# Scatters of half rounds, each half with its own semaphore, and GpSimd's wait two halves back

## The reference

```python
h = relu(layernorm(x));  x = x + rel_gnn(h, 8 relations)      # REL
h = relu(layernorm(x));  x = x + edge_attention(h, 4 heads)   # ATT
h = relu(layernorm(x));  x = x + sage2(h)                     # SAGE0, SAGE1
h = relu(layernorm(x));  x = x + gcn(h)                       # GCN

# the part that all of them share
msg = f(h)[src]                                    # a row per edge
agg = segment_sum(msg, dst, num_segments=50000)    # summed by destination
out = g(h) + agg                                   # a row per node
```

## Time and profile before

| what | value |
|---|---|
| median of 3 runs | 4481.74 us (4466.53 to 4487.24) |
| profiled execution | 4498.36 us, its span 4496.7 us |
| SAGE0's stretch with scatters | 2413 to 2806 us |
| SAGE1's | 3219 to 3688 us |
| GCN's | 4084 to 4480 us |
| busy: PE, DVE, ACT, POOL | 65%, 56%, 43%, 55% |
| packets of SyncE's queue | 233406, 34.5% of the 16 DMA engines' time |
| packets of GpSimd's queue | 90944, 13.2% |

### The profile page before, as it was taken

The page is one execution under the profiler, slowest core; times in us unless marked ns, Lnnn a source line. Parts: engine busy times, 40 slices in busy tenths (PEclk is TensorE's granted clock), DMA queues, the critical chain, the costliest instruction groups (busy, mean ns, idle before and its releaser), DMA issues.

```text
span 4496.7 us, 81538 instructions
## 1 busy us (share of the span) xinstructions
PE 2929.0 (65%) x19724; PEld 2566.6 (57%) x19724; DVE 2499.0 (56%) x11513; ACT 1955.0 (43%) x5394; POOL 2473.3 (55%) x2379
## 2 busy tenths in 40 slices
PE   6888887774656563004767777566777665777666
PEld 5887886663555553003655555466666554666666
DVE  5666667885555453883324555323466563445666
ACT  2222325664544442113546555223444444556555
POOL 5565553666788886445554555545444435554444
PEclk9999998998877776556888676778888887889989
DMA  4444436875333333992113767211277771114767
GB/s 160 157 166 156 163 127 192 239 239 157 41 41 41 41 41 75 313 310 77 38 36 112 229 218 220 71 31 34 86 245 239 230 241 49 37 38 137 221 216 220
DMA packets 328251, 638.77 MB, mean 142 GB/s; under 512 B 61072, under 2 KB 89776, under 8 KB 321992
## 3 DMA queue, kind: packets, MB, share of 16 engines
q1 hardware_dynamic: 233406, 501.99, 34.5%
q0 software_dynamic: 90944, 133.85, 13.2%
q10 hardware_dynamic: 3786, 1.65, 0.1%
HBM read 371.35 MB, written 277.50 MB: 144 GB/s over the span
## 4 chain that ended last, share of the span: by engine, by line
PE 16%; DMA 13%; issue 11%; POOL 10%; another core or an unknown queue 4%; DVE 4%; ACT 3%; SPq 0%; POOLq 0%; DVEq 0%; ACTq 0%
DMA sums<-parked,last_i 12%; POOL sums L774 9%; PE bank L1201 6%; PE bank L1197 3%; PE bank L1185 3%; PE bank L1167 2%; DVE out_stats L1665 1%; PE bank L1137 1%; ACT e_h L911 1%; DVE out_mv L1672 1%; ACT out_sd L1072 1%; ACT psum_out L948 1%; DVE n_t L1765 0%; POOL got L739 0%
## 5 line engine op out<-in xcount | busy, mean ns | idle before, releaser
L774 POOL DMA_INDIRECT sums<-parked,last_i x588 | 603.5, 1026 | 702.6 <-DMA sums<-parked,last_i 506.4
L739 POOL DMA_INDIRECT got<-rows,gidx x588 | 602.7, 1025 | 404.8 <-ACT e_h L911 188.4
L948 ACT ACTIVATE psum_out<-bank 128x132 f32<-128x132 f32 x784 | 219.7, 280 | 939.3 <-remote 455.0
L1201 PE MATMUL bank<-psum_out,eq 128*128 128x132 f32 x1568 | 387.2, 332 | 246.0 <-ACT psum_out L948 154.6
L1033 ACT ACTIVATE n_h<-ring 128x128 f32<-128x128 f32 x1176 | 482.9, 482 | 143.7 <-DMA ring<-rows 71.2
L1302 PE MATMUL bank<-ring,ident 128*128 128x128 f32 x2352 | 507.6, 302 | 0.0
L1201 PEld LDWEIGHTS bank<-psum_out,eq 128*128 128x128 f32 x1568 | 271.2, 216 | 306.4 <-ACT psum_out L948 181.9
L1299 PE MATMUL bank<-w_t,n_ht 128*128 128x128 f32 x1568 | 355.7, 353 | 136.1 <-DMA ring<-sums 135.3
L1277 PE MATMUL bank<-ident,n_h 128*128 128x128 f32 x1176 | 226.9, 324 | 330.9 <-ACT n_h L1033 248.2
L1182 PE MATMUL bank<-parked 128*128 128x128 f32 x3136 | 409.7, 283 | 32.7 <-issue 26.1
L1182 PEld LDWEIGHTS bank<-parked 128*128 128x128 f32 x3136 | 386.9, 199 | 41.4 <-issue 40.6
(11 more groups left out here) (182 smaller groups left out, 7292.4 us busy)
## 6 DMA issues: line engine op xcount, KB each, us to landing
ring<-sums SPq DMA_DIRECT2D x392, 264.0 KB
ring<-rows SPq DMA_DIRECT2D x392, 264.0 KB
rows<-ring SPq DMA_DIRECT2D x294, 264.0 KB
ring<-attsums SPq DMA_DIRECT2D x98, 264.0 KB
rowsg<-ring SPq DMA_DIRECT2D x98, 264.0 KB
ring<-rowsg SPq DMA_DIRECT2D x98, 264.0 KB
sums<-parked SPq DMA_DIRECT2D x16, 1584.0 KB
attsums<-parked SPq DMA_DIRECT2D x16, 1584.0 KB
```

The lines of the kernel that those rows point to most:

```text
L739: pool.indirect_dma_start(out=got[:, b, j, 0:width], out_offset=None, in_=table[:, :], in_offset=bass.IndirectOffsetOnAxis(ap=gidx[:, b, j ...
L774: pool.indirect_dma_start(out=sums[:, :], out_offset=bass.IndirectOffsetOnAxis(ap=last_i[:, t:t + 1], axis=0), in_=parked[:, t, :], in_off ...
L948: nc.scalar.activation(psum_out[:, b, j, :], bank[4 + j % 2][:, 0:W], ACT.Copy)\
L1201: nc.tensor.matmul(o, lhsT=eq[:, b, j, 1, :], rhs=carried, start=False, stop=True)\
```

## The change

The scatter of a round is split in two halves of two tiles. Each half has a semaphore of its own (`half_scattered[0]`, `half_scattered[1]`), which counts 32 for each landed half. GpSimd issues the first half of a round, waits for the second half of the round before, issues the second half, and waits for the first. `rounds_landed` is counted when a round's second half has been waited for. The indices, the data and the number of DMAs are the same, and at most two halves are under way, as four scatters were before.

```diff
+        half_scattered = [Signal(sem(f"half_scattered{q}"), 32) for q in range(2)]
...
-                def round_landed(r):
-                    b = r % 2
-                    pool.wait_ge(scattered[b].sem, (parity_first(seg_index(phase), b) + r // 2 + 1) * 16 * TPR)
-                    pool.sem_inc(rounds_landed.sem, 1)
-
-                def scatter_parked(r):
+                def half_landed(r, q):
+                    pool.wait_ge(half_scattered[q].sem, 32 * (parked_before(phase) + r + 1))
+                    if q == 1:
+                        pool.sem_inc(rounds_landed.sem, 1)
+
+                def scatter_half(r, q):
                     pool.wait_ge(parked_ready.sem, parked_before(phase) + r + 1)
                     gate(pool)
-                    for j in range(TPR):
+                    for j in (2 * q, 2 * q + 1):
                         t = r * TPR + j
                         pool.indirect_dma_start(
                             out=sums[:, :], out_offset=bass.IndirectOffsetOnAxis(ap=last_i[:, t:t + 1], axis=0),
                             in_=parked[:, t, :], in_offset=None,
-                            bounds_check=bound, oob_is_err=False).then_inc(scattered[r % 2].sem, 16)
+                            bounds_check=bound, oob_is_err=False).then_inc(half_scattered[q].sem, 16)
...
                     for r in range(ROUNDS):
-                        scatter_parked(r)
-                        round_landed(r)
+                        scatter_half(r, 0)
+                        if r:
+                            half_landed(r - 1, 1)
+                        scatter_half(r, 1)
+                        half_landed(r, 0)
+                    half_landed(ROUNDS - 1, 1)
```

## The result

The changed kernel took 4708.4 us (median of 4 runs, 4652.75 to 4770.33) beside 4482.27 us for the kernel before (median of 4, 4466.53 to 4487.24). Two of the changed kernel's four, the profiled one among them, lie over 1.5% above the fastest, and the ratio of 1.043 (95% interval 1.037 to 1.048) is of the other two alone, 4652.75 and 4693.18 us. So it is slower, by 191 us by those two and by 226 us by the median of all four, where I forecast 187 us less. The profiled execution took 4723.61 us, its span 4721.9, 225.2 us more than the span before; what follows is read from this one execution. The lines of the changed kernel are those of before plus 1 ahead of the scatters and plus 5 behind them (scatter 775, `load_s` 640, `n_h` 1038, the turn 1282, the products 1304).

A forecast was written before the change was run, and what follows sets the result against it. Scatter landing and issue were taken to bound SAGE0, SAGE1 and GCN, with the node phase next. 48 x ((8.09 - 6.8) + (9.67 - 8.4) + (8.14 - 6.8)) = 187 us off 4481.7 gave 4295, range 4215 to 4390.

The forecast's parts named there:

- What bounds the kernel now: In SAGE0, SAGE1 and GCN the scatters' landing (12%) and issue (9%) are the path, some 944 us; nothing is full.
- The scatter's new period: Time per round of scatters with overlapping halves: 5.40 us in SAGE0, 6.88 in SAGE1, 5.47 in GCN.
- If L stayed: With L, GpSimd's idle time for a landing, unchanged, the scatter gains 2.7 us a round and stops being the bound.
- the landing under load: In SAGE0 a quiet scatter landing of 2.19 us becomes an estimated 4.0 at high load; scatter period 6.4, under 6.8.
- rival (a): Landing grows linearly with DMA share, stays the bound: SAGE0 7.35, SAGE1 8.85, GCN 7.45 us; gain 108 us, 4374; chance 0.30.
- The node phase's period, 1.1 over the floor: Node phase per round at about 1.1 over the higher floor: 6.8 us in SAGE0, 8.4 in SAGE1, 6.8 in GCN.
- the sum: Gains per round in SAGE0, SAGE1 and GCN, added over 48 rounds: 48 x 3.90 = 187 us.
- Rival (b): Node phases of SAGE0, SAGE1, GCN reach their floors, 6.1, 7.63, 6.1 us a round; gain 291 us, 4191; chance 0.07.
- What is late next is the node phase: In SAGE0, SAGE1 and GCN the node phase, no longer the scatter, sets the pace, at 6.8, 8.4 and 6.8 us.
- Rival (d): With bulk traffic never pausing, two halves land later than a round took before: 101 us lost, 4583; chance 0.05.
- the share stays near 0.70 with the scatters early: Sign of a wrong forecast: DMA share near 0.70, an unpriced wait between loads, slots and stores setting the pace.

The follow-up runs named there:

- with three ahead: Kernel before, rounds of four, with GpSimd's wait for a round moved behind the third scatter of the next: 3654.07 us beside 4012.62, ratio 0.910.
- with one ahead: Kernel before, rounds of four, with GpSimd's wait for a round moved behind the first scatter of the next: 3908.73 us beside 4011.69, ratio 0.974.

## Why the prediction was wrong, point by point

*What bounds the kernel now.* Right. The landing and the issue of the scatters were the path, and the three stages where they ran gave all the time that moved.

*The scatter's new period.* Right only on the first chip, where the stalled node phase left the DMA engines nearly idle: 5.29, 6.09, 5.40 us, against 5.40, 6.88, 5.47. In the trace from one of the others it was 6.42, 7.21 and 6.25, since L was longer.

*"If L stayed": the landing under load, rival (a).* It grew, from 2.95, 4.42 and 3.25 us to 3.7, 4.5 and 3.8 in the changed kernel and 4.2, 4.9 and 4.1 with three ahead, and it stayed the bound of the changed kernel, as (a) has it. (Some of the growth may be the chip: with one ahead L was 3.9 in SAGE0 at a share of 0.74.) But it grew far less than by (a)'s line, which gave periods of 7.35, 8.85 and 7.45. With three ahead GpSimd had 3 x (194.39 / 180 + 0.30) + 0.30 = 4.4 us between the last issue of a round and the wait for it, and found it landed in 30 of 48 rounds, at a DMA share of 0.96. The line of rival (a) would have put L at 2.95 + 0.26 x 1.47 / 0.05 = 10.6 us. The Trainium skill, in DMA: Bandwidth & Descriptors, section Queues, rings and completion order, has each DMA engine take turns between queues by packets; landings that climb so little agree with it. The same page, section Latency and other measured facts, has 2 us of memory latency at high load, from which the prediction made an estimated 4.0; the 4.2 of SAGE0 at a share of 0.96 is near it.

*The node phase's period, 1.1 over the floor.* Mis-sized, and these were the terms of the sum, with the wrong bound behind them. I took 6.8, 8.4 and 6.8 and "the scatter itself at 5.4 to 6.9 stays under all three". In the trace from one of the six chips the changed kernel's periods were 6.42, 7.21 and 6.25, and they were the scatter's. With three ahead the node phase did its rounds in 5.84, 6.87 and 5.89 us (SAGE0: (2448.8 - 2165.8) / 97 x 2, from the first and last load of sums). The work per round was right: share times period is 0.88 x 6.42 = 5.65, 0.97 x 7.21 = 6.99 and 0.91 x 6.25 = 5.69 us, against 5.66, 7.25 and 5.78. But a share of 0.95, read from ATT, isn't the ceiling (1.01 was reached), the margin of REL didn't carry over, and of ACT's and PE's 5.8 to 6.7 us a round the 6.7 was a matter of PE's clock, which rose. Rival (b), with 291 us, has the number of these chips, 293, and by luck: in (b) the node phases stand at their floors and set the pace, and here the landing did. The mechanism is (a)'s, the size is (b)'s.

*"What is late next is the node phase", at a pace of its own.* This is the step that failed in the result. It took the node phase's pace to be independent of what GpSimd does meanwhile. On the first chip PE reported a matmul every 2.80 us while GpSimd issued without a break, and 13, 45 and 19 groups of 98 got through. In the kernel before GpSimd fell silent for 2.95 to 4.42 us in every round, and the node phase kept up. That these pauses were what kept it going is argued from the two traces of that kind, where the pause is the thing that changed, and isn't shown: no run with the pauses put back fell on such a chip. Even with them PE wasn't quite on time (in GCN's scatters 31 of 186 recorded updates are 2.0 to 2.9 us late). What holds PE's reports up stays open, the profiler's own records included.

*Rival (d), slower.* It had the sign but not the mechanism. Its halves were to land late; on the first chip GpSimd waited 2.2 us for landings in all of SAGE0. No rival of mine had an engine off the path slowed by the issue itself. And the trace of the kernel before had shown it, in SAGE0's edge phase, on ACT's `psum_out`:

```profile
L948 ACT ACTIVATE psum_out<-bank x195: 275/280/282, 2075.3 to 2419.8; 128x132 f32<-128x132 f32 x195
...
  PE bank L1201: 81.0, 160
  remote: 53.3, 18
```

53.3 us in 18 places until "remote", beside a PE that had long ended, while GpSimd issued gathers. I read the scatter stages closely and of the edge phases one gap between gathers, as the change didn't touch them. With signals up to 14 us late in bursts of issues, a stage of 196 issues without a break should at least have been a rival, on the slower side, with more than 0.05.

Of the signs that I named for a wrong forecast one came, in a stronger form: not "the share stays near 0.70 with the scatters early" but a share of 0.20, and the cause was neither a slot nor a store.

## What to carry to other kernels

A wait that drains a queue each round is worth replacing by one that looks a round back: on the chips without the stall each step further ahead (one, two, three scatters of four) gained, 0.974, 0.923, 0.910, until the DMA share stood at 0.96 or more. But a wait also keeps an engine silent, and what lives in that silence has no row in the profile of before: look in the trace for places where the engine already issues without a break, and see how the others fare there. A gain of 7% on three chips was a loss of 4% on a fourth, so such a change is measured on more than one before it is kept; an idle time until "remote" in a kernel on one core is the first thing to follow up. And a time close to a forecast or a rival isn't yet its mechanism: the chain inside the stage says what still sets the pace.

## What the hardware did that I had not expected

- Two kinds of chip for the same kernel: 4466.5 to 4487.2 us on one, 4006.5 to 4018.3 on six. Nearly all of the difference lies in the edge phases (349 us in the kernel before against 254 for SAGE0's 196 gathers).
- On the first, PE's signals late while GpSimd issued indirect DMAs: 2.80 us for each matmul, in stages with 13 and with 20 of them a group, while ACT's and DVE's signals passed in 0.01 us and SyncE's own instructions went in steps of 0.70 us. Gone within 20 us of the last issue. Whether the stream causes it, and whether it exists without the profiler, no run shows.
- A DMA share of 1.01 and 342 GB/s beside scatters, above the 0.95 and 310 of plain traffic in ATT.
- The landing of a scatter climbs little with the mean load: 2.2 us quiet, 3.8 right after a round at a share of 0.53, 4.2 at 0.96 in SAGE0, 4.9 at 1.01 in SAGE1.
